# A fused recurrent-attention and expert-FFN kernel on one core: shared mixing product in column halves, second mixing factors on array quadrants, instruction order rewritten

## What is computed

```python
xn = layernorm(x)                                   # x: 2 x 2048 x 256
# attention part, 4 heads of 64
dx = shift(xn) - xn;  xm = xn + dx * x_miu
mix = tanh(xm @ x_A).reshape(.., 6, 32)             # x_A: 256 x 192
miu = lambdas + einsum('btgk,gkc->gbtc', mix, x_B)  # x_B: 6 x 32 x 256
r_in, w_in, k_in, v_in, a_in, g_in = xn + dx * miu
v = v_in @ vW.T;  r = r_in @ rW.T;  g = tanh(g_in @ g_A) @ g_B
w, k, a_gate = ...                                  # low-rank products, sigmoids, key norm
# per head, over time: S = S*decay + (S a) b^T + v k^T;  y = S r
out = (groupnorm(y) + bonus) * g @ oW.T
# expert part: route to 2 of 8 low-rank experts, relu, down projection, silu
x + out * silu(ffn(xn))
```

## Time and profile before

| | us |
|---|---|
| median of 3 runs | 1008.69 |
| lowest, highest | 1007.28, 1008.87 |
| the profiled execution | 1008.61 |
| its span | 1006.5 |

### The profile page before, as it was taken

One profiled execution on the slowest core, in us unless ns is written; L12 is line 12 of the kernel. 1 busy time (PEld: TensorE's weight loads), 2 busy tenths in 40 slices (PEclk: granted clock), 3 DMA queues, 4 the chain that ended last, 5 costly groups with the idle time before them and its releaser, 6 DMA issues.

```text
span 1006.5 us, 45425 instructions
## 1 busy us (share of the span) xinstructions
PE 994.1 (99%) x19916; PEld 781.5 (78%) x19916; DVE 845.2 (84%) x1683; ACT 661.4 (66%) x1461; POOL 453.7 (45%) x537
## 2 busy tenths in 40 slices
PE   8999999999999999999999999999999999999998
PEld 6777778777787877778777787777877778787775
DVE  5887979888888888889889898887888888888775
ACT  3656675756767576676666767567575666857655
POOL 3372534535445363543725436353453534436231
PEclk9999999999999999999999999999999999999999
DMA  7000000000000000000000000000000000000000
GB/s 254 12 4 3 3 4 23 4 23 4 3 23 4 23 4 23 3 4 23 4 24 2 3 24 3 23 4 3 23 4 23 3 13 13 3 23 4 13 4 23
DMA packets 9411, 17.13 MB, mean 17 GB/s; under 512 B 1920, under 2 KB 4096, under 8 KB 8960
## 3 DMA queue, kind: packets, MB, share of 16 engines
q1 hardware_dynamic: 9216, 14.23, 4.4%
HBM read 10.03 MB, written 4.19 MB: 14 GB/s over the span
## 4 chain that ended last, share of the span: by engine, by line
PE 91%; DVE 5%; issue 2%; ACT 1%; SPq 0%; DMA 0%; DVEq 0%
PE bank L254 37%; PE bank L253 14%; PE grams L468 10%; PE bank L345 5%; PE grams L537 2%; PE bank L483 2%; PE bank L494 2%; PE bank L527 2%; PE grams L442 2%; PE grams L557 2%; PE grams L592 2%; PE bank L568 2%; PE bank L360 2%; PE bank L376 2%; PE bank L302 2%
## 5 line engine op out<-in xcount | busy, mean ns | idle before, releaser
L1263 POOL TENSOR_TENSOR bk<-bk,tot 128x256 f32<-128x256 f32 x192 | 153.5, 810 | 212.9 <-PE grams L468 212.9
L1576 DVE COPY_PREDICATED gm<-c_mask_g,grams 128x1024 f32<-128x1024 int32 x96 | 160.2, 1668 | 14.3 <-PE grams L468 14.3
L916 ACT ACTIVATE relu<-bank,prm 128x256 f32<-128x256 f32 x256 | 107.2, 470 | 80.7 <-PE bank L254 78.8
L1244 POOL TENSOR_TENSOR xd<-mtmp,xnc 128x512 f32<-128x512 f32 x96 | 120.7, 1271 | 33.7 <-DVE mtmp L1442 33.7
L254 PE MATMUL bank<-xnc,w_wi 128*128 128x256 f32 x512 | 124.4, 386 | 0.0
L468 PEld LDWEIGHTS grams<-ar,bk 64*64 64x64 f32 x6144 | 100.8, 135 | 23.3 <-issue 14.9
L1020 ACT ACTIVATE gl<-gm 32x128 f32<-32x128 f32 x320 | 98.9, 309 | 30.1 <-DVE gm L1576 23.3
L254 PE MATMUL bank<-xmt,w_lora_B 128*128 128x256 f32 x444 | 115.4, 388 | 0.0
L468 PE MATMUL grams<-ar,bk 64*64 64x64 f32 x6144 | 111.8, 221 | 2.7 <-DVE ar L1586 2.4
L254 PEld LDWEIGHTS bank<-xnc,w_wi 128*128 128x128 f32 x512 | 94.6, 190 | 17.7 <-issue 5.0
L1586 DVE TENSOR_TENSOR ar<-ar,tot 128x512 f32<-128x512 f32 x96 | 92.9, 967 | 15.9 <-PE grams L468 15.7
(11 more groups left out here) (230 smaller groups left out, 2221.9 us busy)
## 6 DMA issues: line engine op xcount, KB each, us to landing
x_in<-x SPq DMA_DIRECT2D x16, 256.0 KB, 2.8
out<-out_t SPq DMA_DIRECT2D x15, 256.0 KB, 2.0
w_wi<-w_wi_dram SPq DMA_DIRECT2D x1, 1024.0 KB, 6.6
w_wo<-w_wo_dram SPq DMA_DIRECT2D x1, 1024.0 KB, 9.1
w_lora_B<-w_lora_B_dram SPq DMA_DIRECT2D x1, 512.0 KB, 8.5
w_x_A<-w_x_A_dram SPq DMA_DIRECT2D x1, 256.0 KB, 2.7
w_x_B<-w_x_B_dram SPq DMA_DIRECT2D x1, 256.0 KB, 2.8
w_kW<-w_kW_dram SPq DMA_DIRECT2D x1, 256.0 KB, 3.9
```

The lines of the kernel that those rows point to most:

```text
L916: A(dst[:, p % 2, j * 256:(j + 1) * 256], ZB[p % 2][:, j * 256:(j + 1) * 256], ACT.Relu, bias=prm[:, P_BI + 2 * p + j:P_BI + 2 * p + j + 1 ...
L1244: tt(xd[:, q, :, :], mtmp[:, k % 2, :, :], xnc[steps["front"] % 2][:, :, :], ALU.add).then_inc(S(f"xd_{k}_done"), 1)
L1263: tt(v, v, d, ALU.mult).then_inc(S(f"bk{k}_scaled"), 1)
L1576: run(v.copy_predicated(dst, msk.to_broadcast([128, 32, HALF // m, m]), src), "g_stored")
```

## The change

1. `mix`: x_A has 192 columns; before they were padded to 256 and multiplied as two full-width blocks. Now the first 128 are done in column halves, and the last 64 as 64-column matmuls on both column halves at once, each for one half of the tokens.
2. `miu`: x_B and the mixed factors are laid out with 64 rows for each of the six products (the padding rows are zero), and each product is computed in 64*64 quadrants; two products and two column halves are in the array together. Before, each was a 32*128 matmul. `mixt_e` now has five activations (one of 128x256, four of 32x128) in place of two, and `mixt` is zeroed once at the start.
3. The lists of all engines are reordered, with other banks (`USED_BY`) and other choices of full width or halves.
4. The last step: its list is reordered, `last_zt(1)` has a bank of its own, and `last_out` writes into `zz`, not into `out_t`, so that it no longer waits for the store of the tile before; `last_fgate` waits for `o_read`.

```diff
@@ -58,8 +58,9 @@
         for p in range(PAIRS)}
 POSTS = {"ysg_done", "fgate_done", "zt_mm", "zt_done", "o_mm", "o_read", "out_done", "out_stored"}
 
-USED_BY = {"xt": 3, "route": 4, "mix": 3, "wk_A": 4, "kW": 3, "wk_B": 4, "norm": 3, "a_A": 4, "keys0": 3, "r":
-           4, "a_B": 3, "g_A": 4, "zt": 3, "keys1": 4, "xmt": 3, "o": 4, "bonus": 3, "g_B": 4, "v": 3}
+USED_BY = {"xt": 3, "route": 4, "mix": 3, "wk_A": 4, "kW": 3, "wk_B": 4, "g_A": 3, "zt": 4, "norm": 3, "keys0":
+           4, "r": 3, "a_A": 4, "a_B": 3, "bonus": 4, "keys1": 3, "o": 4, "v": 3, "xmt": 4, "g_B": 3,
+           "last_zt": 3}
 FIRST_USED_BY = {"xt": 0, "route": 2, "mix": 1, "kW": 5, "wk_A": 6, "g_A": 0, "wk_B": 2, "a_A": 1, "a_B": 5, "norm":
            6, "r": 0, "v": 2, "g_B": 1, "xmt": 5, "bonus": 6}
@@ -330,20 +331,22 @@
 
             def mix(half=False):
                 pe.wait_ge(*till("xm_done", 2))
-                for u in range(2):
-                    for c in range(2):
-                        last = mm2(half, used_by("mix")[:, u * 256:(u + 1) * 256], w["x_A"][:, c, u * 128:(u + 1) * 128], xm[:, c, :],
+                for c in range(2):
+                    mm2(True, used_by("mix")[:, 0:256], w["x_A"][:, c, 0:128], xm[:, c, :], start=(c == 0), stop=(c == 1))
+                for c in range(2):
+                    for o in (0, 64):
+                        last = mm(used_by("mix")[o:o + 64, 256:384], w["x_A"][:, c, 128:192], xm[:, c, 2 * o:2 * o + 128],
                                   start=(c == 0), stop=(c == 1))
                 last.then_inc(S("mix_mm"), 1)
 
             def miu(pair):
-                pe.wait_ge(*till("mixt_done", 2))
+                pe.wait_ge(*till("mixt_done", 5))
                 for c in range(2):
-                    for k in (2 * pair, 2 * pair + 1):
-                        q = MIX_ORDER[k]
-                        o, u = 32 * (q % 4), q // 4
-                        last = mm(MIU[k % 2][:, c * 256:(c + 1) * 256],
-                                  w["x_B"][o:o + 32, u, c * 128:(c + 1) * 128], mixt[o:o + 32, u, :], start=True, stop=True)
+                    for o in (0, 64):
+                        for k in range(2):
+                            r, u = 64 * k, pair % 2
+                            last = mm(MIU[k][o:o + 64, c * 256:(c + 1) * 256], w["x_B"][r:r + 64, pair, c * 128 + o:c * 128 + o + 64],
+                                      mixt[r:r + 64, u, :], start=True, stop=True)
                 last.then_inc(S("miu_mm"), 1)
 
             def low(name, q, m, half):
 
             def last_zt(g):
                 pe.wait_ge(S("last_zz_done"), g + 1)
-                if g:
-                    pe.wait_ge(*till("zt_done", 1))
-                    pe.wait_ge(*till("bkt_done", 1))
                 for c in range(2):
-                    last = tr((used_by("zt") if g else CB)[:, c * L:(c + 1) * L], zz[:, g, c * 128:(c + 1) * 128], ident[:])
+                    last = tr((used_by("last_zt") if g else CB)[:, c * L:(c + 1) * L], zz[:, g, c * 128:(c + 1) * 128], ident[:])
                 last.then_inc(S("last_zt_mm"), 1)
 
...
                 else:
                     if rec:
                         base(1)
-                        lora(1)
                         barrier(step)
                         gram(0)
+                        lora(1)
                         base(0)
-                        lora(0)
-                    if front:
-                        if full:
-                            pe.wait_ge(*till("v_done", 0))
-                        xt_()
-                    if rec:
-                        diff(1)
                     if front:
                         if full:
                             pe.wait_ge(*till("gate_done", 0))
-                        route()
-                    if rec:
+                        xt_()
+                    if rec:
+                        diff(1)
+                        lora(0)
                         gram(1)
-                        diff(0)
...
-                        if rec:
-                            pe.wait_ge(*till("bkt_done", 2))
-                        elif front:
-                            pe.wait_ge(*till("hg_done", 1))
-                        elif full:
-                            pe.wait_ge(*till("gate_done", 0))
-                        o_(half=True)
-                    if front:
-                        pe.wait_ge(*till("xmt_done", 1))
-                        bonus_()
+                        v_(half=True)
                         diag(rec)
+                    if rec:
+                        down(3)
+                        down(2, final=True)
+                    if front:
                         if post:
                             pe.wait_ge(*till("o_read", 1))
-                        elif rec:
-                            pe.wait_ge(*till("bkt_done", 2))
                         else:
-                            pe.wait_ge(*till("hg_done", 1))
+                            pe.wait_ge(*till("bonus_done", 1))
+                        xmt_()
+                        pe.wait_ge(*till("v_done", 3))
                         g_B()
-                        pe.wait_ge(*till("bonus_done", 1))
-                        v_()
                 if step == 1:
@@ -933,7 +931,10 @@
             def mixt_e():
                 act.wait_ge(*till("mix_mm", 1))
                 A(mixt[:, 0, :], used_by("mix")[:, 0:256], ACT.Tanh).then_inc(S("mixt_done"), 1)
-                A(mixt[0:64, 1, :], used_by("mix")[0:64, 256:512], ACT.Tanh).then_inc(S("mixt_done"), 1)
+                for r in range(2):
+                    for o in (0, 64):
+                        A(mixt[64 * r:64 * r + 32, 1, 2 * o:2 * o + 128], used_by("mix")[o + 32 * r:o + 32 * r + 32, 256:384],
+                          ACT.Tanh).then_inc(S("mixt_done"), 1)
 
             def xmt_e():
                 act.wait_ge(*till("xmt_mm", 1))
@@ -1676,13 +1683,13 @@
 
             def last_fgate():
                 dve.wait_ge(S("last_ysg_done"), 1)
+                dve.wait_ge(S("o_read"), TILES - 1)
                 need(run(v.tensor_tensor(fgate[:, :, :], y1[:, :, :], ysg[:, :, :], ALU.mult)))
 
             def last_out(g):
                 dve.wait_ge(S("last_o_mm"), g + 1)
-                dve.wait_ge(S("out_stored"), 16 * (TILES - 1))
-                need(run(v.tensor_tensor(out_t[:, g, :], GB[g][:, 0:C], fgate[:, g, :], ALU.mult)))
-                run(v.tensor_tensor(out_t[:, g, :], out_t[:, g, :], x_in[(TILES - 1) % 4][:, g, :], ALU.add), "last_out_done")
+                need(run(v.tensor_tensor(zz[:, g, :], GB[g][:, 0:C], fgate[:, g, :], ALU.mult)))
+                run(v.tensor_tensor(zz[:, g, :], zz[:, g, :], x_in[(TILES - 1) % 4][:, g, :], ALU.add), "last_out_done")
 
             def zz_(step, post):
                 dve.wait_ge(*till("yn_done", 1))
@@ -1931,11 +1944,12 @@
     par[:, P_XMIU:P_XTIME] = cols(a["attn_x_miu"])
     par[:, P_XTIME:P_BI] = cols(a["attn_x_time"])
     par[:, P_BI:P_COLS] = cols(a["ffn_bi"])
-    x_b = np.zeros((128, 2, 256), np.float32)
-    x_b[:, 0, :] = a["attn_x_B"][:4].reshape(128, 256)
-    x_b[0:64, 1, :] = a["attn_x_B"][4:].reshape(64, 256)
+    x_b = np.zeros((128, 3, 256), np.float32)
+    for pair, places in enumerate((((W_, 32), (K_, 64)), ((A_, 0), (G_, 64)), ((R_, 0), (V_, 96)))):
+        for q, row in places:
+            x_b[row:row + 32, pair, :] = a["attn_x_B"][q]
     weights = {
-        "x_A": np.pad(halves(a["attn_x_A"]), ((0, 0), (0, 0), (0, 64))), "x_B": x_b,
+        "x_A": halves(a["attn_x_A"]), "x_B": x_b,
```

373 lines of the change are left out of this document (198 added, 175 removed).

## The result

The changed kernel took 995.36 us (median of 4 runs, 992.79 to 996.91) against 1007.99 of the kernel before on the same chip: a ratio of 0.9871, 95% interval [0.9859, 0.9884]. The forecast was 984.3 in a range of 978 to 997. Sign and range held; of the 24 us that the working gave, 12.6 came. The time lies in the range that I had given to rival B (989 to 1003), and not in that of the forecast itself (980 to 990). The profiled execution took 996.0, 2.1 over its span of 993.9.

The account below looks back on a forecast made before the run. PE's instruction list, almost never waiting, was taken as the bound: -1.66 us a step plus 0.25 for new waits, -1.40 times 15 is -21.0; with -3.3 in the last step, 1008.6 becomes 984.3 us, range 978 to 997.

Parts of the forecast that it names:

- rival B: Full steps: PE's shorter list runs into late elementwise engines, 0.4 to 0.9 each, 989 to 1003 us; chance 0.21.
- Parts 1 and 2: Per full step: three miu blocks as quadrants save 0.20 each, -0.60; mix's second column block in side-by-side pairs, -0.43.
- Part 3: Shape changes between neighbouring PE blocks in a full step fall from 2.55 to 2.20, -0.35 us.
- its four places: miu(0), gram(2), gram(4) and inv_x(4), whose producers had about 0.6, 0.6, 0.5 and 0.5 us to spare.
- Part 4: Two old PE waits go in each full step, at route for xnc and a_A for the inverse: -0.28 us.
- the new waits: 0.25 us a full step allowed for PE waiting on producers that become late, bounds 0 and 0.9.
- The last step: The wait ahead of gram(2) is filled and the clock stays full: -3.3 us, bounds -4.2 and -1.
- the border: At the border before the last step, PE's wait of 0.28 for ACT's v_e goes, which is now early.
- about -4.2: Sum of the last step's terms in us, before the allowance for doubt that made it -3.3.
- signs of being right: Period 59.7 to 60.3, miu to gram 0.86 to 0.91, mix 1.3, PE busy 99%, full last-step clock, blocks ≤0.3 over price.
- Rivals C: At the step border, DVE's late y1_, zz_ and ypre make PE wait; slower than before, 1017 us; chance 0.04.
- D: Half-array and quadrant passes in miu and mix don't run side by side; 1026 us; chance 0.02.

Follow-up runs that it names:

- `arrays_only`: The kernel before, in its own order on every engine, with only the new forms of mix and miu and what they need: 1003.63 us, ratio 0.9959.
- experiment 6: The changed kernel with ACT's first rows of the last step in the order of the kernel before, relu(1, 1) behind pack_gram(0): 993.13 us, ratio 0.9851.

## Why the prediction came out as it did

**Parts 1 and 2 (`miu`, `mix`)** were right in place: 1.30 and 0.91 to 0.96 as worked out. As terms to be summed they were wrong. The forms alone give 0.49 a step in the old order (60.86) and the order alone gives nothing (61.36 against 61.35); together they give 1.27 (60.09). A quadrant block is only cheap beside others of its shape: in `arrays_only` the two blocks around `mix` pay 0.10 each for the new neighbour, which eats most of the 0.28 that `mix` gains there.

**Part 3 (neighbours)** was mis-sized. The undisturbed step is 60.08 and not 59.7. Of the 0.38, about 0.3 has a place: `wk_B` takes 1.02 where I had priced 0.05 for its new neighbour, since it now stands ahead of 32x32 tiles and not of a Gram block (0.06); `rec_y(0)` 0.56 and `keys_to_tokens(1)` 0.59 (0.05 each); `route` 0.98 instead of 0.92 (0.06); and `miu(2)` with `gram(4)`, 0.09. The last is a wait: in 12 of the 14 steps `gram(4)` starts 0.26 after POOL's `scale_bk(3, 1)` ends, and in step 16 0.30. In step 12, where PE came 0.2 later against POOL, the distance is 0.43, and there `miu(2)` and `gram(4)` take 1.96 together instead of 2.05. PE in that step, then POOL in step 13, after:

```profile
662.16 1.09 PE L348 MATMUL bank<-mixt,w_x_B 64*64 64x256 f32 x16
663.08 1.11 PE L470 MATMUL grams<-ar,bk 64*64 64x64 f32 x64
664.12 1.13 PE L255 MATMUL bank<-xmt,w_lora_B 128*128 128x256 f32 x4
```

```profile
722.79 1.17 POOL L1265 TENSOR_TENSOR bk<-bk,tot 128x256 f32<-128x256 f32 x1
...
725.48 1.22 POOL L1265 TENSOR_TENSOR bk<-bk,tot 128x256 f32<-128x256 f32 x2 [0.28 <-PE grams L470]
```

The same instruction takes 0.61 alone (two in 1.22) and 1.17 where DVE's `scale_ar(3)` (722.77, 0.68) has begun just ahead of it. So rival B's mechanism is there, at one of its four places and on the other engine, for 0.09 a step. By the Trainium skill, "SBUF — State Buffer", "Who interferes with whom", it waited for the whole of the DVE instruction; the row agrees, with 0.56 more where 0.66 of DVE's instruction was left.

**Part 4 and the new waits.** The two old waits went. The sum of new ones, 0.25 forecast, is 0.34 a step by the trace (0.43 with the 0.09 above). That the size is near was luck: I looked for late producers, and the stalls are late code. What I read from the profile could have told me: the queue of kind "instruction" stands on the page of before with 159 packets, and blocks of 32x32 tiles use up 64 instructions in 0.38 us (730.98 to 731.36 in the timeline above; the same before). The Trainium skill, "Runtime: NRT & Kernel Launch", "Instruction fetch mechanics", does say that code comes in 16 KiB blocks of 256 instructions; it calls the cost of a border mostly hidden. Most of it is hidden here too: of 154 borders in the full steps of the changed kernel five show. Where it isn't hidden it cost up to 1.26 us (`arrays_only`, step 5).

**The last step** gave +0.44 (51.01 to 51.45 from `gram(0)` on) where I had -3.3. The wait of the earlier trace rows went from 2.04 to 0.84 and not to nothing, and `gram(2)` comes 0.83 later than before, since ACT's `relu(1, 1)` now stands ahead of the table load, the sigmoid and `pack_gram(0)`: a moved row on another engine that I had not followed. The clock of the earlier trace rows did stay up there, and fell some 20 us later instead, for 1.5. (The page before shows a full clock in all 40 slices; the dip of 3.4 us is lost in slices of 25.) My 1.7 for the dip before was also high: the executions of the kernel before with a mean granted clock of 0.998 took 1008.2 to 1008.9, those with 0.999 or 1.000 took 1006.9 to 1007.7. Without wait and dip (experiment 6) the step ends at 49.1, so at most 1.9 of the 3.3 were to be had. In that kernel `gram(5)` starts 2.5 earlier than before, and the stretch from there to the end is 0.65 longer, where I had 0.4. The working is also short of itself: the filled wait (1.73), the clock (1.7) and the border (0.28), less 0.4, make 3.3, and for the 0.9 more of "about -4.2" it names no price.

**Step 2** has no output projection between, so `rec_inc(1)` waits 1.28 for ACT's keys there; I had counted 15 equal steps, and this one lost 0.4 instead of gaining 1.4. The 0.95 by which the first `gram(0)` comes earlier is bookkeeping: `lora(1)` (0.96) stood ahead of it and now stands behind. At the other end the kernel before already had the last step's `lora(1)` behind `gram(0)`, which is most of the reason why its step 16 takes 60.84.

Sum, from the spans: start and step 2 -0.6, steps 3 to 16 -12.5, the last +0.44, together -12.6. The forecast for the same three was -1.4, -19.6, -3.3. What is missing is the undisturbed step before all, whose prices of neighbours were too low (0.38 x 14 = 5.3, the wait of 0.09 among it), then the last step (3.7), step 2 with the start (0.8), the stalls beyond 0.25 (0.09 x 14 = 1.3), and 0.5 by the last full step, which was 0.5 under the others in the kernel before. So the range held, but its upper part, meant for late producers, was filled by mis-sized terms and by late code. Of the signs of being right, the period, `miu` and `mix` came; PE busy at 99% (98%) and the full clock in the last step did not.

B's late producers cost 0.09 a step, although the time lies in B's range. Rivals C and D did not come: DVE's step ends at 760.0 and `gram(0)` starts at 761.1 without a wait, and the quadrants run side by side.

## What to carry to other kernels

A stall inside a block of equal instructions, at an instruction that waits for nothing, is not a producer's: number the engine's instructions and see whether the stalls share a place modulo the size of a code packet. In a loop written out, the number of instructions in a step decides which steps are hit, so compare kernels by the undisturbed step and by the stalls apart; a kernel that shows none may only have been lucky. The gain of a smaller array shape and that of its neighbours are one term, to be priced for the order in which the blocks will stand.
